# Four gated residual layers on one core: all five engine streams in a new order, VectorE's sums and aggregations apart

## The reference

```python
x = x + tanh(g_xattn[0]) * L0_xattn(ctx, ctx, layernorm(x))   # A: 16 heads of 16
x = x + tanh(g_ffn[0])   * L0_ffn(layernorm(x))               # B
x = x + tanh(g_xattn[1]) * L1_xattn(layernorm(x), ctx)        # C: one key/value head for 16 query heads
x = x + tanh(g_ffn[1])   * L1_ffn(layernorm(x))               # D

# A: k, q, v of 16 heads from ctx, layernorm(x), ctx
score = einsum('bhij,bhkj->bhik', k, q) / sqrt(dh)
attn  = softmax(score, axis=1)                                # over the HEADS
out   = einsum('bhik,bhij->bhjk', attn, v);  res = out @ Wo.T + Wo_b
# B: (silu(x @ wg.T) * (x @ wu.T)) @ wd.T, 768 hidden columns, weights scaled by 1/127
# C: q = x @ Wq; k, v = split(ctx @ Wkv); softmax over the keys; y @ Wo
# D: x @ W.T + b + x @ (up_aux @ (lora_up @ (lora_down @ down_aux))).T
```

## Time and profile before

| | us |
|---|---|
| three runs | 2436.21, 2441.13, 2443.69 |
| median | 2441.13 |
| the profiled execution, device time | 2435.5 |
| its span on the core | 2433.5 |
| PE busy | 2346.0 (96%), 27814 instructions |
| DVE busy | 2204.6 (91%), 3678 instructions |
| POOL busy | 1775.4 (73%), 2512 instructions |
| ACT busy | 1719.5 (71%), 3402 instructions |

### The profile page before, as it was taken

How to read it: one execution, slowest core, us unless ns; L and a number is a source line. 1 busy time by engine, 2 the same in 40 slices (tenths; PEclk the granted TensorE clock), 3 DMA queues, 4 the chain that set the end, 5 groups by cost and what they waited for, 6 DMA issues and landing times.

```text
span 2433.5 us, 70142 instructions
## 1 busy us (share of the span) xinstructions
PE 2346.0 (96%) x27814; PEld 2069.6 (85%) x27814; DVE 2204.6 (91%) x3678; ACT 1719.5 (71%) x3402; POOL 1775.4 (73%) x2512
## 2 busy tenths in 40 slices
PE   6899999999999999999999999999999999999897
PEld 5788888888888888888888888888888888888786
DVE  6879999999999999999999999999999999999963
ACT  4467777777777777777777777777777777777664
POOL 3667777777787787787777777777777778777653
PEclk9999999999999999999999999999999999999999
DMA  3000010010010011011000001001001001101000
GB/s 106 25 19 29 29 33 26 29 35 24 29 35 29 24 35 30 25 32 30 29 29 30 29 29 31 28 29 35 24 29 35 24 28 35 30 24 33 17 19 15
DMA packets 74326, 73.26 MB, mean 30 GB/s; under 512 B 6555, under 2 KB 73393, under 8 KB 74290
## 3 DMA queue, kind: packets, MB, share of 16 engines
q1 hardware_dynamic: 74290, 72.75, 9.6%
HBM read 54.90 MB, written 16.78 MB: 29 GB/s over the span
## 4 chain that ended last, share of the span: by engine, by line
PE 64%; DVE 20%; ACT 7%; POOL 6%; issue 2%; DMA 0%; POOLq 0%; SPq 0%; DVEq 0%; ACTq 0%
PE work L2135 13%; PE work L2136 11%; PE work L2137 11%; DVE m L1516 6%; PE scores L2228 6%; PE scores L2238 6%; PE work L2271 5%; DVE scores L1522 4%; PE work L2174 4%; ACT e L856 3%; POOL zt L416 3%; PE scores L2217 3%; ACT xn_D L813 3%; PE work L2152 2%; PE work L2158 2%
## 5 line engine op out<-in xcount | busy, mean ns | idle before, releaser
L856 ACT ACTIVATE e<-scores 120x1024 f32<-120x1024 f32 x512 | 514.2, 1030 | 83.7 <-PE scores L2238 52.5
L2135 PE MATMUL work<-xt_hi_B,w_hi 128*128 128x256 f32 x1536 | 453.2, 295 | 4.2 <-DVE y_lo_A L1496 1.6
L2136 PE MATMUL work<-xt_lo_B,w_hi 128*128 128x256 f32 x1536 | 426.7, 278 | 0.0
L2137 PE MATMUL work<-xt_hi_B,w_lo 128*128 128x256 f32 x1536 | 426.6, 278 | 0.0
L416 POOL TENSOR_TENSOR zt<-e 120x512 f32<-120x512 f32 x256 | 328.9, 1286 | 115.8 <-ACT e L856 111.8
L410 POOL TENSOR_TENSOR h_lo<-h_f,h_hi 128x256 fp32r<-128x256 f32 x384 | 280.3, 737 | 146.3 <-ACT h_hi L806 146.2
L1516 DVE TENSOR_REDUCE m<-scores 120x128 fp32r<-120x2048 f32 x128 | 290.9, 2273 | 65.7 <-PE scores L2228 65.6
L2135 PEld LDWEIGHTS work<-xt_hi_B,w_hi 128*128 128x128 f32 x1536 | 289.5, 188 | 62.7 <-DVE h_f L1510 24.9
L1522 DVE TENSOR_TENSOR scores<-scores,m 120x1024 f32<-120x1024 f32 x256 | 302.8, 1227 | 4.3
L1534 DVE TENSOR_TENSOR e<-e,work 120x2048 f32<-120x2048 f32 x128 | 291.1, 2274 | 0.2
L2136 PEld LDWEIGHTS work<-xt_lo_B,w_hi 128*128 128x128 f32 x1536 | 289.9, 189 | 0.0
(11 more groups left out here) (256 smaller groups left out, 7283.2 us busy)
## 6 DMA issues: line engine op xcount, KB each, us to landing
x_ln<-xp SPq DMA_DIRECT2D x64, 256.0 KB, 2.7
x_res<-xp SPq DMA_DIRECT2D x64, 256.0 KB, 2.7
y<-y_out SPq DMA_DIRECT2D x64, 256.0 KB, 2.2
ctx_f_A<-cp SPq DMA_DIRECT2D x64, 128.0 KB, 2.5
ctx_f_C<-cp SPq DMA_DIRECT2D x64, 128.0 KB, 2.0
qm<-mT SPq DMA_DIRECT2D x256, 4.0 KB
e<-wi SPq DMA_DIRECT2D x3, 768.0 KB, 6.7
w_ctx<-wc SPq DMA_DIRECT2D x1, 656.0 KB
```

Of the source, the lines that this page charges most:

```text
L856: return act.activation(e[0:SC, c, 2 * h:2 * h + 2, :, :].rearrange("p a b n -> p (a b n)"), scores[0:SC, 2 * h:2 * h + 2, :].rearrange("p ...
L2135: pe.matmul(out, a_hi, b_hi_, start=first, stop=False, skip_group_check=parts)
L2136: pe.matmul(out, a_hi, b_lo_, start=False, stop=False, skip_group_check=parts)
L2137: last = pe.matmul(out, a_lo, b_hi_, start=False, stop=end, skip_group_check=parts)
```

## The change

Each of the five streams has a new order, in prologue, loop and epilogue. `DEPTH` is 7 in place of 6, so the loop has 57 passes and one batch more is handled outside it; this goes with a loop that is cut at another place: a pass began before wo1 of C and begins now before f1 of D, and f1 belongs to a batch one older (`store_y(t - 7)`).

- **TensorE's loop** is now: f1 of D, gate_up 0 to 2, scores1(0), transposes C, gate_up 4 and 3, scores1(1), attended1(0), attended0 twice, attended1(1), scores0(0), keys_values1, gate_up 5, queries of C, down 0 and 1, wo1 of C, down 2 and 3, key_scores(1), down 4 and 5, wo0 of A, key_scores(0), values0, transposes D, queries of A, scores0(1), transposes B, keys0, maxima_transposed, transposes A.
- **ScalarE** takes the queries of A out (`query_out("A")`) only when scores0(1) is done (`A1_mm`), ahead of `xt_B`, and from there to the first tanh runs `xt_B`, `xt_hi_B`, the odd keys, `mT`, `xt_hi_A`, the even keys, one exponential, `y_out`, the other exponential, tanh 0 and tanh 1.
- **VectorE's** `moments` is taken apart into `sums`, `counted` (the copy) and `mean_variance`. In the loop, layers B, C and D still have the three in a row with the wait between. For layer A `sums` stands after `gated(3)`, `mean_variance` seven instructions later behind `queries_to_columns`, and neither wait nor copy is left. In prologue and epilogue the three are apart at some places. Copies in the whole program: 256 before, 191 now.
- **SP** loads x for the residual one pass later relative to the loop's count, the context of C behind `kv1_mm`, stores the result behind it, loads the context of A behind `v0_mm`, and spreads the maxima last.
- Work banks and semaphores are renumbered to suit. The matmuls of a pass are the same in number and shape. The filling matmuls are 96 in the prologue and 175 in the epilogue.

```diff
-DEPTH = 6
+DEPTH = 7
...
-            def moments(st, x, t):
+            def sums(st, x):
                 for i in range(NT):
                     last = dve.bn_stats(stats[st][:, i, :], x[:, i, :])
-                last.then_inc(s[f"ln_mom_{st}"], 1)
-                dve.wait_ge(s[f"ln_mom_{st}"], within(0, 1, t))
-                dve.tensor_copy(ln_count[:, :], stats[st][:, 0, 0:1])
+                return last
+            def counted(st):
+                return dve.tensor_copy(ln_count[:, :], stats[st][:, 0, 0:1])
+            def mean_variance(st):
                 for i in range(NT):
                     last = dve.bn_aggr(mv[st][:, i, :], stats[st][:, i, :])
                 return last
...
             with nc.scalar.Fori(FIRST + DEPTH, LAST + 1) as t:
...
+                keys0_even(W[2]).then_inc(s["kz0_even"], 1)
+                act.wait_ge(s["A1_sub"], 2 * t + 1)
+                exponential(e0, 1, 0).then_inc(s["A1_exp"], 1)
+                act.wait_ge(s["f1_mm"], t)
+                act.wait_ge(s["st_out"], 16 * t)
+                act.activation(y_out[:, :, :], two(W[0], NT), ACT.Copy).then_inc(s["f1_out"], 1)
+                act.wait_ge(s["A1_sub"], 2 * t + 2)
+                exponential(e0, 1, 1).then_inc(s["A1_exp"], 1)
+                act.wait_ge(s["G_mm0"], t)
+                tanh(0, W[3]).then_inc(s["G_tanh0"], 1)
...
                 act.wait_ge(s["ln_rstd_B"], t)
                 ln_apply("B", x1).then_inc(s["ln_B"], 1)
...
+                act.wait_ge(s["A1_mm"], t)
+                query_out("A", W[1]).then_inc(s["q_out_A"], 1)
                 act.wait_ge(s["T_mm_B"], t)
+                transposed_out("B", W[0]).then_inc(s["T_out_B"], 1)
                 act.wait_ge(s["T_out_B"], t)
+                transposed_hi("B").then_inc(s["T_hi_B"], 1)
+                act.wait_ge(s["k0_mm"], t)
+                keys0_odd(W[2]).then_inc(s["ends_act"], 1)
                 act.wait_ge(s["mT_mm"], t)
+                act.activation(mT[:, :], W[3][:, 0:S], ACT.Copy).then_inc(s["mT_out"], 1)
                 act.wait_ge(s["T_mm_A"], t)
+                transposed_hi("A", W[1]).then_inc(s["T_hi_A"], 1)
...
             with nc.vector.Fori(FIRST + DEPTH, LAST + 1) as t:
...
+                dve.wait_ge(s["T_hi_A"], t)
+                transposed_lo("A", W[1]).then_inc(s["T_lo_A"], 1)
+                dve.wait_ge(s["T_lo_A"], t)
+                reciprocal0(W[1], 0).then_inc(s["ends_dve"], 1)
+                dve.wait_ge(s["G_tanh0"], t)
+                gated(0, W[3]).then_inc(s["G_a0"], 1)
...
             with nc.sync.Fori(FIRST + DEPTH, LAST + 1) as t:
+                load_x_res(t - 3)
                 load_x_ln(t)
-                sp.wait_ge(s["res_A"], t)
-                load_x_res(t - 2)
+                sp.wait_ge(s["kv1_mm"], t)
+                load_ctx("C", t - 4)
+                sp.wait_ge(s["res_D"], t)
+                store_y(t - 7)
                 sp.wait_ge(s["v0_mm"], t)
                 load_ctx("A", t - 1)
-                sp.wait_ge(s["mT_out"], t)
+                sp.wait_ge(s["mT_out"], t + 1)
                 maxima_rows()
```

More of the change, by code:

```diff
@@ L2138, in product @@
                     first = False
-                if bias is not None:
-                    last = pe.matmul(out, bias[0], bias[1], start=False, stop=True)
                 return last
@@ new lines, in _ @@
+            transposes(W[1], "A").then_inc(s["T_mm_A"], 1)
+            keep_busy(W[0], 12)
+            pe.wait_ge(s["A1_exp"], 12)
+            scores0(0).then_inc(s["A0_mm"], 1)
+            keep_busy(W[0], 5)
+            pe.wait_ge(s["A0_p"], 5)
+            attended0(W[0], 0)
+            pe.wait_ge(s["A1_p"], 5)
+            attended0(W[0], 1).then_inc(s["yA1_mm"], 1)
+            keep_busy(W[3], 8)
+            pe.wait_ge(s["yA_lo"], 5)
+            rows_out(W[3], y_hi["A"], y_lo["A"], "wo0").then_inc(s["woA_mm"], 1)
@@ L2389, in _ @@
[L2389 to L2396 removed]
+            queries(W[3], "A", "q0").then_inc(s["ends_pe"], 1)
+            pe.wait_ge(s["v0_pad"], 5)
@@ new lines, in _ @@
+            down(W[0], 3)
+            down(W[0], 4)
+            pe.wait_ge(s["G_lo5"], 6)
+            down(W[0], 5).then_inc(s["dn_mm5"], 1)
+            pe.wait_ge(s["yA_lo"], 6)
+            pe.wait_ge(s["kz1_even"], 7)
+            rows_out(W[3], y_hi["A"], y_lo["A"], "wo0").then_inc(s["woA_mm"], 1)
+            queries(W[1], "A", "q0").then_inc(s["ends_pe"], 1)
+            transposes(W[2], "A").then_inc(s["T_mm_A"], 1)
+            pe.wait_ge(s["A0_exp"], 14)
+            scores0(1).then_inc(s["A1_mm"], 1)
@@ L2397, in _ @@
+            pe.wait_ge(s["G_lo4"], 7)
+            down(W[3], 4)
+            pe.wait_ge(s["G_lo5"], 7)
+            down(W[3], 5).then_inc(s["dn_mm5"], 1)
+            pe.wait_ge(s["A0_exp"], 16)
+            key_scores(1).then_inc(s["M1_mm"], 1)
+            pe.wait_ge(s["yA_lo"], 7)
+            rows_out(W[1], y_hi["A"], y_lo["A"], "wo0").then_inc(s["woA_mm"], 1)
+            pe.wait_ge(s["res_B"], 7)
+            values0(W[3]).then_inc(s["v0_mm"], 1)
             pe.wait_ge(s["M1_max"], 7)
@@ new lines, in _ @@
+            pe.wait_ge(s["G_lo5"], LAST + 1)
+            down(W[0], 5).then_inc(s["dn_mm5"], 1)
+            rows_out(W[2], y_hi["A"], y_lo["A"], "wo0").then_inc(s["woA_mm"], 1)
+            pe.wait_ge(s["M1_max"], LAST + 1)
+            key_scores(0).then_inc(s["M0_mm"], 1)
+            values0(W[1]).then_inc(s["v0_mm"], 1)
+            pe.wait_ge(s["ln_D"], LAST + 1)
+            pe.wait_ge(s["res_B"], LAST + 1)
+            transposes(W[0], "D").then_inc(s["T_mm_D"], 1)
+            queries(W[3], "A", "q0").then_inc(s["ends_pe"], 1)
```

3675 lines of the change are left out of this document (1958 added, 1717 removed), and 9 rows, old and new, of tables (given, passing).

## The result

The changed kernel takes 2361.07 us (median of four runs, 2358.72 to 2361.89) against 2442.07 us of the kernel before beside it: a ratio of 0.9671, 95% interval 0.9653 to 0.9689. The forecast of 2412 us, 1.2% faster, had the sign right and less than half of the size; the range ended at 2390. The profiled execution took 2358.72 us at a span of 2356.9, 76.6 us less than the 2433.5 of before.

A forecast was written before the change was run, and what follows sets the result against it. It took a ring of ScalarE to the first tanh, then VectorE, to set the pass at 35.63 us against 36.16: 57 x -0.53 = -30.2, plus 1.6 for fillers, span 2404.9, forecast 2412 us, range 2390 to 2450.

The forecast's parts named there:

- The transposes of D: TensorE's stall ahead of them, waiting for ScalarE's xn_D, goes when they move behind wo0 of A: 0.42 us a pass.
- TensorE's switches: Entries from 32-row matmul groups to products: three fewer a pass at 0.10 us each, TensorE's work 35.70 to 35.40 us.
- rival 3: Faster: TensorE sets the pass at 35.40 us, ScalarE's part being 0.23 shorter than counted; 2399 us, chance 0.07.
- The new ring: ScalarE from scores0(1) to first tanh 7.08 us, then VectorE 28.55: pass 35.63, with VectorE waiting about 1.0 at the tanh.
- What bounds the kernel: Order at one or two places decides; TensorE 35.70 us and VectorE 34.68 of a 36.16 us pass, neither with much room.
- The copy: VectorE's copy for A, one of four in the loop, goes: 0.07 us a pass, 4.0 us if VectorE sets the end.
- Prologue and epilogue: 13 more fillers cost 1.6 us; the ramps' waits otherwise taken as zero change, bound 15 us either way.
- Rival 4: Prologue clock: with 41 fillers fewer the low-clock stretch could double, 5 us more; 2417 us, chance 0.05.
- Rivals 1 and 2: 1: ScalarE chain behind scores0(1) doesn't overlap, 2458 us, chance 0.17; 2: waits only move, only copy saved, 2439 us, 0.17.

The follow-up runs named there:

- first experiment: Kernel before with D's transposes moved behind wo0 of A and key_scores(0) ahead of values0 on TensorE: 2523.37 against 2434.55 us, ratio 1.0362.
- tenth: Changed kernel with only D's transposes back at their old place, ahead of wo0 of A: 2575.82 us, ratio 1.0547 to the kernel before.
- seventh: Changed kernel with three filling products between two groups of 32-row matmuls, ahead of attended1(1): 2410.13 us against 2437.47 of the kernel before, ratio 0.9885.
- third: Changed kernel with ScalarE's y_out in the loop copied in four pieces of 128x128 instead of one: 2371.07 us, ratio 0.9740 to the kernel before.
- sixth: Kernel before with D's layer norm earlier on VectorE, queries of C ahead of the second exponential on ScalarE, D's transposes unmoved: ratio 1.0295.
- thirteenth: Changed kernel with A's copy, mean and variance back behind its sums in the loop, with the wait: 2362.01 us against 2435.17 of the kernel before, ratio 0.9701.
- eighth: Changed kernel with A's mean and variance ahead of VectorE's wait for attended1(1) and D's copy removed: 2363.98 us against 2437.47 of before, ratio 0.9697.
- fourth: Changed kernel with one more maximum over 384 columns on VectorE each pass, ahead of the residual of C: 2377.82 us, ratio 0.9767 to the kernel before.
- fourteenth: Kernel before with A's moments, root and xn moved behind B's on VectorE, GpSimd and ScalarE, TensorE's order unchanged: ratio 1.0045.
- fifth: Kernel before with D's transposes behind wo0 of A, key_scores(0) ahead of values0, and GpSimd's root of B ahead of xt_lo of D: ratio 1.0310.

## Why the prediction was wrong in size

Two terms of the sum failed, each with about half of the miss: the length of a pass, put at 35.63 us and measured at 35.24, and prologue and epilogue, put at nothing and measured at 24 us less.

- **The transposes of D.** "I take the stall as gone: 0.42 us" held; from start to start the stall was 0.50 us (0.79 us from key_scores to the transposes, where 0.29 is usual). The reason given, that enough products stand ahead of them, was incomplete: in the old order they also gave y_lo of A its time (first experiment), and the move costs 89 us there, while going back costs 210 us in the new order of the other engines (tenth).
- **TensorE's switches.** "At 0.10 for each of the three, TensorE's own work is ... 35.40 us" failed. From the start of each matmul to that of the next, averaged over 50 passes:

| us a pass | before | after |
|---|---|---|
| from the last matmul of one kind to the first of the next (24 changes, 22 after) | 5.15 | 4.15 |
| of that, the wait named above | 0.50 (xn_D) | 0.19 (key_max) |
| inside runs of one kind | 31.00 | 31.09 |
| own steps, without that wait | 35.65 | 35.05 |

  So TensorE's own steps fell by 0.60 us, not 0.30, and its waits by 0.31: together the 0.92 of the pass. Of the 0.60, 0.51 is at the groups of 32-row matmuls: the changes into and out of them fell from 3.03 to 2.32 us, those between two kinds of 32-row matmul rose from 0.70 to 0.90. The prediction missed the price, since such a group costs at both ends (0.22 us in the seventh), and also the count: in the order of a pass there are as many runs between the groups as groups, six before and five after, where it has "from seven to five". A step of 0.18 us behind A's transposes, where 0.03 is usual, went as well, but one of 0.25 between f1 of D and gate_up 0 came, where 0.11 is usual. The floor of 35.40 was too high, and with it rival 3's 2399 us.
- **The new ring.** "Ring: 7.08 + 28.55 = 35.63" was the right mechanism at too long a time. From the end of scores0(1) (1219.43 + 1.17) to gated(0) at 1227.41 it is 6.81 us, and the rest of VectorE's pass 35.24 - 6.81 - 0.19 = 28.24: together 35.05, where the prediction has 7.08 and 28.55. That is 0.19 less than the pass, by VectorE's wait for the attended values; but by attended0 the same ring had as little as 0.03 us to spare (third). So it runs level with TensorE and does not stand 0.23 above it. VectorE's wait was 0.46, not 1.0.
- **What bounds the kernel.** The prediction read waits one by one, and not the chain that closes on itself. By the chain view the old pass was a ring through four engines, of which the stall was one symptom. The sixth, made to shorten that ring, brought two longer waits instead, so this stays a reading.
- **The copy.** 4.0 us was taken. The thirteenth and eighth runs show no worth that can be told: at this place VectorE's wait for the attended values takes the copy up. More work elsewhere on VectorE does lengthen the pass (fourth). As to the rule that the prediction sets against its 0.07 us: the section it names adds that an operation that is not held starts earlier, so that the row and the Trainium skill ("VectorE: DVE Perf Modes", "The DRAIN you can't avoid") need not differ.
- **Prologue and epilogue.** "I take zero", 15 us either way, failed: 76.6 - 57 x 0.925 = 23.9 us by the prediction's way of counting. Most of it is the epilogue's new order (27 of 33 us without its fillers). The prediction counted the fillers as a cost of 1.6 us; taking the epilogue's 175 out cost 4.5. Rival 4's clock was 0.98, no worse.
- The miss of 51 us: 57 x (0.925 - 0.53) = 22.5 for the pass, 23.9 + 1.6 = 25.5 for the ramps, and 3.2 because the profiled execution of the changed kernel lay 2.4 under its median, not 5.6.

Rivals 1 and 2 did not happen; rival 3, TensorE as the bound, came nearest, from a floor that was still 0.35 us too high. What stays open is how much of the 0.92 us each part of the new order gives: five edits in the old order, one alone or several together, each made it slower (the fourteenth by 0.45% only), so no part was found that gives any of it alone. Fewer groups of 32-row matmuls, which the steps above point to, were not tried by themselves in the old order.

## What to carry to other kernels

When five in-order streams wait for each other, follow the chain of waits until it closes on itself and count that ring; a stall may be where the ring shows and not a piece that can be taken out. A step moved past such a stall must be checked for whom its old place gave time to, on every engine behind it. Where rings are of nearly the same length, as here, single moves can all make things worse, and a re-ordering of all streams can still win.

## What the runs showed that was not expected

- Three filling products took 0.44 us of TensorE's steps inside a run of products and 0.66 between two groups of 32-row matmuls; the pass grew by 0.43 and 0.89, 0.2 of the latter in slower product steps elsewhere.
- With a stall of 2.5 us once in a 39 us pass the mean granted clock of the loop was 0.97; with stalls of 0.6 to 0.9 us (first, fifth, sixth) it stayed at 1.00.
- Taking out the prologue's 96 fillers lowered the granted clock there from 0.97 to 0.93 and the time not at all.
